# Dense stage: a unit's shift, normalising and the turn of x one pair later; scatter stage: normalising of y with a second load buffer

## The reference

```
h = relu(layernorm(x))
for m in range(3):                                  # attention layers
    g = h @ W[m]; s = g @ a_src[m]; d = g @ a_dst[m]
    e = leaky_relu(s[src] + d[dst])                 # edges and one self loop per node
    alpha = softmax of e over the edges of one dst
    h = h + sigmoid(segment_sum(alpha * g[src], dst) + bias[m])
y = x + h
h = relu(layernorm(y))
for m in range(3):                                  # edge layers
    ee = edge_attr @ enc_w[m] + enc_b[m]
    agg = segment_sum(h[dst] with ee, src)          # and one self loop per node
    z = relu(batchnorm(agg @ w1[m] + b1[m]))
    h = z @ w2[m] + b2[m]                           # relu after layers 0 and 1
return y + h
```

## Time and profile before

| | us |
|---|---|
| time, median of 3 runs | 12837.08 |
| lowest and highest | 12827.12, 12846.73 |
| the profiled execution | 12854.73 |
| its span | 12853.1 |
| POOL busy in the span | 6444.5 (50%) |
| TensorE busy | 7017.4 (55%) |
| VectorE busy | 5349.2 (42%) |
| ScalarE busy | 4324.3 (34%) |

### The profile page before, as it was taken

The page is one execution under the profiler, slowest core; times in us unless marked ns, Lnnn a source line. Parts: engine busy times, 40 slices in busy tenths (PEclk is TensorE's granted clock), DMA queues, the critical chain, the costliest instruction groups (busy, mean ns, idle before and its releaser), DMA issues.

```text
span 12853.1 us, 167790 instructions
## 1 busy us (share of the span) xinstructions
PE 7017.4 (55%) x35048; PEld 5096.5 (40%) x35048; DVE 5349.2 (42%) x23215; ACT 4324.3 (34%) x9423; POOL 6444.5 (50%) x5862
## 2 busy tenths in 40 slices
PE   5666666750277007732222377774336887444888
PEld 2333335640266006621111255553224555333666
DVE  5666666651366226643333344441112333111544
ACT  5666663320133005532222244441113444111444
POOL 6666663456555656665666432335663333665000
PEclk9888887875688558855555688985557898555999
DMA  4555554445443555556666665666666777444998
GB/s 154 173 176 172 172 178 121 129 133 189 159 129 127 178 182 167 169 145 157 152 153 153 172 203 202 206 202 173 153 153 190 230 233 224 69 59 87 276 274 270
DMA packets 2016182, 2199.58 MB, mean 171 GB/s; under 512 B 235717, under 2 KB 1404889, under 8 KB 2009712
## 3 DMA queue, kind: packets, MB, share of 16 engines
q1 hardware_dynamic: 1698698, 1822.96, 43.4%
q0 software_dynamic: 308896, 372.55, 14.7%
q10 hardware_dynamic: 8390, 2.21, 0.1%
HBM read 1093.42 MB, written 1119.97 MB: 172 GB/s over the span
## 4 chain that ended last, share of the span: by engine, by line
DMA 18%; issue 11%; PE 10%; DVE 6%; another core or an unknown queue 5%; SPq 3%; POOL 2%; ACT 1%; POOLq 0%; DVEq 0%; ACTq 0%
DMA agg_d<-dO,fOI 11%; PE ps L1407 5%; DMA bXd<-agg_d 4%; PE ps L1394 2%; PE ps L1384 2%; DMA agg_d<-dO,dOI 2%; DMA aX<-y_d 2%; POOL bO L902 1%; SPq L653 1%; DVE aO L2004 1%; DVE uBS L1895 1%; DVE bXd L1977 1%; POOL agg_d L893 1%; PE ps L1382 1%
## 5 line engine op out<-in xcount | busy, mean ns | idle before, releaser
L954 POOL DMA_INDIRECT bXs<-x_d,fGI x784 | 794.7, 1014 | 1546.4 <-DMA x_d<-aH 1334.4
L893 POOL DMA_INDIRECT agg_d<-dO,fOI x784 | 1211.0, 1545 | 648.2 <-ACT dO L1082 417.7
L1082 ACT COPY dO<-ps 128x128 f32<-128x128 f32 (+1 forms) x1176 | 318.2, 271 | 2942.3 <-DMA agg_d<-dO,fOI 1644.7
L1394 PE MATMUL ps<-aS,W1X 128*128 128x512 f32 x2352 | 1206.4, 594 | 0.7 <-DMA eET<-eaT_d 0.7
L1407 PE MATMUL ps<-W,aT 128*128 128x128 f32 x9408 | 1190.3, 288 | 23.2 <-ACT aS L1116 15.9
L2012 DVE TENSOR_TENSOR aH<-ps,B 128x512 f32<-128x512 f32 x588 | 406.4, 692 | 1894.4 <-PE ps L1407 1163.4
L1363 PE MATMUL ps<-bO,bNE 128*128 128x128 f32 x1568 | 577.4, 476 | 1129.5 <-ACT dO L1082 1114.9
L1407 PEld LDWEIGHTS ps<-W,aT 128*128 128x128 f32 x9408 | 1165.6, 205 | 40.1 <-ACT aS L1116 26.3
L1122 ACT ACTIVATE aT<-ps,BNT,BNS 128x512 f32<-128x512 f32 x1176 | 881.3, 774 | 587.7 <-PE ps L1395 556.9
L1181 PE MATMUL ps<-aT,W 128*128 128x512 f32 x1176 | 776.1, 763 | 480.0 <-DVE aT L1570 382.4
L847 POOL DMA_INDIRECT bXs<-x_d,bGI x784 | 785.2, 1001 | 365.7 <-issue 248.2
(11 more groups left out here) (283 smaller groups left out, 17685.3 us busy)
## 6 DMA issues: line engine op xcount, KB each, us to landing
agg_d<-zeros SPq DMA_DIRECT2D x788, 256.0 KB
bXd<-agg_d SPq DMA_DIRECT2D x784, 256.0 KB
agg_d<-zeros SPq DMA_DIRECT2D x394, 290.0 KB
bXd<-agg_d SPq DMA_DIRECT2D x392, 290.0 KB
x_d<-aO SPq DMA_DIRECT2D x392, 256.0 KB
aX<-y_d SPq DMA_DIRECT2D x392, 256.0 KB, 4.0
x_d<-aH SPq DMA_DIRECT2D x392, 256.0 KB
aX<-x_d SPq DMA_DIRECT2D x392, 256.0 KB
```

Source lines behind the costliest of these rows:

```text
L893: pool.indirect_dma_start(agg_d[m][u % 2], bass.IndirectOffsetOnAxis(ap=index, axis=0), dO[:, u, 0:AW[m]], None, bounds_check=agg_last, oo ...
L954: pool.indirect_dma_start(fX[:, s, u, 0:C], None, gin_in[m], bass.IndirectOffsetOnAxis(ap=fGI[:, s, u:u + 1], axis=0), bounds_check=n_last ...
L1394: pe.matmul(z, W1X[:, m, h * P:(h + 1) * P], eHT[:, k, :], start=True, stop=False)
```

## The change

In the dense stage:

- DVE computes a unit's shift (`unit_shift`) at the start of the next pair instead of near the end of the pair of its statistics. `shift` of the next pair of tiles moves ahead of `unit_stats`.
- ACT normalises the first half of a unit before the sigmoids of m = 0 and the second half behind them; the next pair's `normed` moves from behind the sigmoids of m = 2 to behind those of m = 1.
- TensorE transposes the next pair (`a_turn`) between the back transposes of m = 1 and m = 2 instead of at the end.
- POOL's order in a pair is four gathers, `a_rstd`, three gathers, `u_rstd`, one gather.

In the scatter stage y goes to two buffers in turn, `bXs` and `aX`. SP loads the first two rounds at the start, and in round i, when the rows of round i - 1 are written, the y of round i + 1, ahead of the stores of round i - 1. Each buffer has its own semaphore. DVE, ACT and SP run these rounds by `b_rounds` (three unrolled, two per loop iteration, two unrolled); POOL and TensorE keep their loops. POOL waits once, after the stage, until all rows of y are written, since `bXs` is used again.

The diff (lines that only rename or regroup semaphores are left out):

```diff
@@ scatter stage: buffers
+        gX = [bXs[:, :, :, :].rearrange("p s u c -> p (s u c)").rearrange("p (t j c) -> p t j c", t=4, j=J), aX]
...
+        g_in = sems("g_in", 2)
@@ -600,9 +602,9 @@
                              attr[bass.ds(r * (U * P), U * P), :].rearrange("(u p) c -> p u c", p=P)
                              ).then_inc(d_at, 16 * U)
 
-            def g_load(i):
+            def g_load(i, b):
                 for t in range(4):
-                    sp.dma_start(aX[:, t, :, :], tile_of(4 * i + t)(y_d)).then_inc(g_in, 16)
+                    sp.dma_start(gX[b][:, t, :, :], tile_of(4 * i + t)(y_d)).then_inc(g_in[b], 16)
 
             def g_store(i):
                 for t in range(4):
@@ -623,21 +625,25 @@
                         zero_tile(m, b, t)
 
             sp.wait_ge(s_dclr, 1)
-            attr_round(0)
-            g_load(0)
-            layer_zeros(1, 0)
-            with sp.Fori(1, R - 1) as i:
-                sp.wait_ge(d_acc, U * i)
-                attr_round(i)
-                g_store(i - 1)
-                g_load(i)
+            def d_round(i, s, n):
+                if isinstance(i, int) and i == 0:
+                    attr_round(0)
+                    for b in range(2):
+                        g_load(b, b)
+                else:
+                    sp.wait_ge(d_acc, U * i)
+                    if isinstance(i, int) and i == R - 1:
+                        sp.wait_ge(d_at, 16 * U * (R - 1))
+                        attrs(R - 1, (R - 1) * U)
+                    else:
+                        attr_round(i)
+                        sp.wait_ge(g_n, 4 * J * i)
+                        sp.sem_inc(s_gate, 1)
+                        g_load(i + 1, 1 - s)
+                    g_store(i - 1)
                 layer_zeros(1, i)
-            sp.wait_ge(d_acc, U * (R - 1))
-            sp.wait_ge(d_at, 16 * U * (R - 1))
-            attrs(R - 1, (R - 1) * U)
-            g_store(R - 2)
-            g_load(R - 1)
-            layer_zeros(1, R - 1)
+
+            b_rounds(sp, d_round)
             g_store(R - 1)
             zeros_left(1)
 
@@ -811,13 +817,13 @@
 
             def a_pair(p, q, n, unit):
                 first, last = pair_ends(p)
-                u_gather(unit(0), 0, 2)
+                u_gather(unit(0), 0, 4)
                 if not last:
                     a_rstd(p + 1)
-                u_gather(unit(0), 2, 5)
+                u_gather(unit(0), 4, 7)
                 if unit(1):
                     u_rstd(unit(1))
-                u_gather(unit(0), 5, U)
+                u_gather(unit(0), 7, U)
 
             pool.wait_ge(s_setup, 1)
             a_rstd(0)
@@ -930,6 +936,7 @@
             for u in range(U):
                 d_add(R - 1, u)
 
+            pool.wait_ge(g_n, 4 * J * R)
             for m in range(1, M):
                 f0 = [(m - 1) * RS[s] for s in range(2)]
 
@@ -1008,6 +1015,8 @@
 
             def a_pair(p, q, n, unit):
                 first, last = pair_ends(p)
+                if unit(2):
+                    unit_normed(unit(2), 0, U // 2)
                 for m in range(M):
                     for k in range(2):
                         act.wait_ge(a_mm, 2 * M * p + 2 * m + k + 1)
@@ -1018,10 +1027,11 @@
                             act.wait_ge([a_s1, a_s2][m - 1], 32 * (p + 1))
                             act.copy(aO[:, k, m - 1, :, :], ps[4 + k][:, :].rearrange("p (j c) -> p j c", j=J)
                                      ).then_inc(a_o, 1)
-                    if m < 2 and unit(2):
-                        unit_normed(unit(2), m * U // 2, (m + 1) * U // 2)
+                    if m == 0 and unit(2):
+                        unit_normed(unit(2), U // 2, U)
+                    if m == 1 and not last:
+                        normed(p + 1, 1 - q)
                 if not last:
-                    normed(p + 1, 1 - q)
                     by_channel(p + 1)
 
             normed(0, 0)
@@ -1074,34 +1084,34 @@
 
 
             for m in range(M):
-                def d_round(r, m=m):
+                def d_round(r, s=0, n=0, m=m):
                     for u in range(U):
                         act.wait_ge(d_acc, U * r + u + 1)
                         if not isinstance(r, int) or r > 0:
                             act.wait_ge(d_a[u % 2], 16 * ((U // 2) * (r - 1) + u // 2 + 1))
                         act.copy(dO[:, u, 0:AW[m]], ps[2 + u % 4][:, 0:AW[m]]).then_inc(d_o, 1)
                         if m == 0 and u < 4 and past(r - 1):
-                            g_rows(r - 1, u)
+                            g_rows(r - 1, u, 1 - s)
                     if m == 0:
                         act.wait_ge(g_mv, r + 1)
                         act.activation(gSQ[:, :], gVE[:, :], ACT.Sqrt).then_inc(g_sq, 1)
 
-                def g_rows(i, t):
+                def g_rows(i, t, b):
                     if t == 0:
                         act.wait_ge(g_nm, i + 1)
                         if past(i - 1):
                             act.wait_ge(g_st, 64 * i)
                     for j in range(J):
-                        act.activation(aYG[:, t, j, 0:C], aX[:, t, j, :], ACT.Relu, bias=gNM[:, J * t + j:J * t + j + 1],
+                        act.activation(aYG[:, t, j, 0:C], gX[b][:, t, j, :], ACT.Relu, bias=gNM[:, J * t + j:J * t + j + 1],
                                        scale=gRS[:, J * t + j:J * t + j + 1]).then_inc(g_n, 1)
 
                 if m == 0:
-                    d_round(0)
-                with act.Fori(1 if m == 0 else 0, R) as i:
-                    d_round(m * R + i)
-                if m == 0:
+                    b_rounds(act, d_round)
                     for t in range(4):
-                        g_rows(R - 1, t)
+                        g_rows(R - 1, t, 0)
+                else:
+                    with act.Fori(0, R) as i:
+                        d_round(m * R + i)
 
 
                 n0 = m * NT
@@ -1198,8 +1208,8 @@
                         if m < M - 1:
                             a_mul(p, m + 1, k)
                         a_back(p, m, k)
-                if not last:
-                    a_turn(p + 1)
+                    if m == 1 and not last:
+                        a_turn(p + 1)
 
             a_turn(0)
             a_rounds(pe, a_pair)
@@ -1571,22 +1581,22 @@
 
             def a_pair(p, q, n, unit):
                 first, last = pair_ends(p)
+                if unit(2):
+                    unit_shift(unit(2))
                 for k in range(2):
                     add(p, 0, k)
                 if not last:
                     a_stats(p + 1, 1 - q, n + q)
                 for k in range(2):
                     add(p, 1, k)
+                if not last:
+                    shift(p + 1)
                 if unit(1):
                     unit_stats(unit(1))
                 if unit(-3):
                     unit_index(*unit(-3)[:4])
-                if not last:
-                    shift(p + 1)
                 for k in range(2):
                     add(p, 2, k)
-                if unit(1):
-                    unit_shift(unit(1))
                 if unit(3):
                     unit_dots(unit(3))
                 for k in range(2):
@@ -1885,14 +1896,14 @@
 
                     return 0 if isinstance(i, int) and i == 0 else 10 * i - 4
 
-                def g_stats(i, step):
-                    v.wait_ge(g_in, 64 * (i + 1))
+                def g_stats(i, b, n, step):
+                    v.wait_ge(g_in[b], 64 * (n + 1))
                     if past(i - 1):
                         v.wait_ge(g_nm, i)
                     v.sem_inc(s_gate, 1)
                     for t in range(4):
                         for j in range(J):
-                            ins = v.bn_stats(gBS[:, J * t + j, :], aX[:, t, j, :])
+                            ins = v.bn_stats(gBS[:, J * t + j, :], gX[b][:, t, j, :])
                     step(ins)
                     v.sem_inc(s_gate, 1)
                     for w in range(4 * J):
@@ -1914,7 +1925,7 @@
                     v.scalar_tensor_tensor(out=gNM[:, :], in0=gMV[:, :, 0], scalar=-1.0, in1=gRS[:, :], op0=ALU.mult,
                                            op1=ALU.mult).then_inc(g_nm, 1)
 
-                def d_round(i, m=m, g_stats=g_stats, g_scale=g_scale, step_base=step_base):
+                def d_round(i, s=0, n=0, m=m, g_stats=g_stats, g_scale=g_scale, step_base=step_base):
                     r = m * R + i
                     if m == 0:
                         step = steps(d_c, step_base(i), 10)
@@ -1943,7 +1954,7 @@
                         v.wait_ge(d_ix, i + 1)
                     v.wait_ge(d_s, U * (r + 1))
                     if m == 0:
-                        g_stats(i, step)
+                        g_stats(i, s, n, step)
                         for u in range(U):
                             v.wait_ge(d_g[u], 16 * (r + 1))
                         v.sem_inc(s_gate, 1)
@@ -1962,9 +1973,7 @@
```

(4 more changed lines are left out.)

4 lines of the change are left out of this document (2 added, 2 removed).

## The result

The changed kernel takes 12502.12 us (median of 4 runs, 12496.71 to 12511.0), the kernel before 12839.89 us beside it (4 runs): ratio 0.9739, 95% interval 0.9722 to 0.9756. The forecast was 12641 us with 12560 to 12780. It is faster, as forecast, but by 338 us instead of 196, and outside the range. The execution profiled after has a span of 12502.3 us (12853.1 before).

What follows compares the result with a forecast made beforehand. Waits between engines were taken as the bound: dense on POOL's chain, scatter on `dGI` held by late y. Dense +32 and scatter -228 gave -196 us, so 12641 us, range 12560 to 12780.

Steps and rivals of the forecast that it cites:

- What bounds each stage: Dense: pair's end hangs on POOL (aMV, aRS, three gathers, uRS, dots); scatter: POOL waits 278.5 us for `dGI`.
- The dense chain: Dense stage: new order followed from t = 0, pairs closing after 18.7 and 20.3 us, against 18.80 and 20.37.
- two new waits: Dense stage: DVE waits for ACT's sigmoids, about 2.5 us at the pair's head and 1.5 before the m = 2 adds.
- The price of a loop's turn: Dense stage: DVE's loop-turn idling now stands before the shift, 1.3 us per four pairs, +32 us.
- 0.1 less: Dense stage: forecast shortening of a pair's period in us, 10 us over the stage.
- which I count as nothing: Dense stage: the 10 us gain from shorter periods was entered as 0, beside the steps' uncertainty.
- The scatter gap: Scatter stage: POOL's 5.98 us idle before a round's first gather falls to 0.30, saving at most 265 us.
- What gives some back is that SP's transfers bunch: Scatter stage: 16 transfers leave together instead of 12, delaying landings by 0.8 us a round, 37 us.
- Rival 1: Dense stage keeps part of the removed `uRS` wait as gain, 145 us less, total 12464 us; chance 0.11.
- Rivals 2 and 3: Scatter stage: 2, transfers eat the gain, 12793 us, chance 0.14; 3, landings wait behind all bulk writes, 12894 us, 0.07.
- rival 4: Scatter stage: y was not what held `dGI`, the gathers would have; 12869 us, chance 0.04.
- three signs of being wrong: Pairs under 18.5 us on average, eighth add's wait over 6 us, or round's first add waiting over 2 for `dOI`.

Runs made afterwards that it cites:

- stores-first run: Changed kernel with y's loads put back behind the stores, both buffers kept: 11659.28 us, ratio 0.9759 to the kernel before, scatter stage 1416.0 us.

## Why the forecast was right and wrong

1. **What bounds each stage** was right: taking the wait for `uRS` away gave the dense stage nothing to speak of, and y had held `dGI`.
2. **The dense chain** was right step by step, within 0.5 us at each of its eight points, and so were its two new waits (2.5 to 2.7 and about 1.5 us forecast, 2.39 and 1.75 measured). The price of a loop's turn was too low: the pairs that hold it take 19.92 us on average where they took 18.81, and beside the ordinary gain of 0.55 that is 1.7 more for 1.3 forecast, 41 us over the stage. But the three other pairs of four came out shorter than "0.1 less": 17.99, 19.72 and 19.87 us on average against 18.45, 20.15 and 20.64, 0.55 a pair and 54 us over the stage. Together -13, which is what was measured. The step that failed is "which I count as nothing": the term of 0 was 0.55 us a pair. In the pair shown the chain runs 0.2 to 0.3 us ahead at its end.
3. **The scatter gap** was right: 5.98 became 0.30.
4. **"What gives some back is that SP's transfers bunch"** is the step that failed, in its sign, and it put the total out of the range. The forecast counted transfers in the burst (16 for 12), took longer landings and gave 37 us back. The landings got shorter (medians 6.24 to 4.84 us for the sixth add, 6.61 to 5.56 for the eighth), and POOL idles 1.2 us a round less ahead of the last two adds. Over 47 intervals that is 57 us gained, and 37 + 57 are the 94 by which the term was too small. What counts is the order in which SP issues, shown by the stores-first run: the same transfers in the old order give the old landings and a stage 70 us longer. What in the order does it, the zero fills queued close behind the loads or the store just ahead of them, stays open.
5. **The Trainium skill** has two rules on this on the page "DMA: Bandwidth & Descriptors", section "Queues, rings and completion order". By the one, transfer engines take turns between queues packet by packet; by the other the write that raises the semaphore lands only after every earlier write of its engine, across its queues. By the first the prediction put the 37 us near 0, and they were below it. No run here decides between the two: the transfer engines were 0.90 busy while the sixth add was under way before and 0.84 after, for 5.73 and 5.06 us, and for the eighth add 8 more zero fills queued went with 5.56 instead of 4.64 us.
6. **Rivals.** Rival 1's time, 12464, is nearest to the measured one, but by chance: it laid 145 us on the dense stage, which gave 13. Rivals 2 and 3 made the transfers dearer and fell; rival 4 fell with the gap. No case allowed the burst to become cheaper. I had bounded the dense term below nothing and this one only at nothing, and the range was short on that side. None of the three signs of being wrong came up (pairs of 19.36 us on average, an eighth wait of 1.9, no wait for `dOI`), since for this stage they looked only for dearer landings; what did miss were the 3 to 4 us expected for the eighth add's wait and the round of 29.8.

## What to carry to other kernels

When a change adds transfers to a queue that one engine issues in order, write down the new order of issue beside the instruction that waits for a landing, and ask what is moving and what is queued at that moment; their number alone misled here. Before giving a wait's time to a chain, look at what the engine that releases it had been given just before: here the eight normalisations moved ahead of the m = 2 sigmoids, with TensorE's turn, cost 177 us and hid most of the worth of the edit. Price a moved stretch from both sides of nothing.

## What the runs showed of the hardware

- A scatter-add of 128 rows lands in 3.4 to 3.5 us when no bulk transfer is near (medians), in 4.7 to 5.0 when four loads of 256 KB are issued right behind it and stores follow, in 6.1 to 6.2 when a store stands ahead of the loads and zero fills follow at once, and in 6.4 to 6.9, at most 8.0, when loads are issued up to 3 us ahead of it.
- Transfers issued by one engine moved in the order of issue: in the changed kernel the stores' 512-byte packets begin when about nine tenths of the loads' 2 KB packets have gone (458 of 512, median of 44 rounds).
- Four chips ran the same kernel in 11949 to 12840 us. The two stages bound by waits between engines and by landings took the same time on each within about 1%; the difference lay elsewhere (3030 against 3600 us between them, 5260 against 5610 behind). A time saved in such a stage is the same in microseconds within some 10 us, and so another ratio on each chip.
- DVE's idling at the turn of a loop, 1.8 to 2.1 us, cost 0.2 us beside a load (pairs of 18.84 against 18.60 us, medians) and nearly its whole length in front of a chain (20.22 against 18.28).
